# SyncE's reads and stores of finished chunks stand behind the load of pair 36

## The reference

```
x = x + attention(layernorm(x))                       # 16 heads, causal
t = layernorm(x).reshape(4096, 128)
scores = softmax(t @ gate_w.T)                        # 8 experts
_, idx = top_k(scores + gate_bias, 2)
for e in range(8):
    h = silu(t @ w1[e].T) * (t @ w3[e].T)
    y += gate_e[:, None] * (h @ w2[e].T)              # gate_e: the token's weight for e, or 0
z = silu(t @ sw1.T) * (t @ sw3.T) @ sw2.T             # shared experts, all tokens
return x + y + z
```

## Time and profile before

| what | value |
|---|---|
| median of 3 runs | 751.32 us (749.77 to 751.38) |
| the profiled execution, its own time | 750.16 us |
| its span, first to last instruction | 747.3 us |
| mean granted TensorE clock | 0.965 |
| PE, DVE, ACT, POOL busy, share of the span | 83%, 72%, 64%, 62% |

### The profile page before, as it was taken

How to read it: one execution, slowest core, us unless ns; L and a number is a source line. 1 busy time by engine, 2 the same in 40 slices (tenths; PEclk the granted TensorE clock), 3 DMA queues, 4 the chain that set the end, 5 groups by cost and what they waited for, 6 DMA issues and landing times. The chain is left out here.

```text
span 747.3 us, 27456 instructions
## 1 busy us (share of the span) xinstructions
PE 620.2 (83%) x10116; PEld 468.1 (63%) x10116; DVE 537.0 (72%) x1836; ACT 474.7 (64%) x987; POOL 465.7 (62%) x536
## 2 busy tenths in 40 slices
PE   4676978899798999897999988899988678879581
PEld 2354656677576767675677766667765456657461
DVE  7865777788687799886879887888974465425372
ACT  2686977788688868887877887977662232313210
POOL 9453454655446667868655887756587256777652
PEclk9988999999999999999999999999999899989986
DMA  9899998778998876987877886886552534333583
GB/s 255 258 278 321 335 311 261 241 218 257 305 280 248 252 221 185 275 272 206 259 217 217 237 258 211 261 252 190 179 195 66 144 110 108 106 96 105 139 249 86
DMA packets 150227, 161.89 MB, mean 217 GB/s; under 512 B 13676, under 2 KB 115825, under 8 KB 149776
## 3 DMA queue, kind: packets, MB, share of 16 engines
q1 hardware_dynamic: 145488, 151.67, 68.0%
q0 software_dynamic: 4608, 8.47, 3.3%
HBM read 93.87 MB, written 67.26 MB: 216 GB/s over the span
## 5 line engine op out<-in xcount | busy, mean ns | idle before, releaser
L1171 DVE CUSTOM_DVE_ANT_0 ps<-ps,near 128x128 f32<-128x128 f32 (+3 forms) x512 | 244.3, 508 | 73.9 <-PE ps L920 59.3
L1091 ACT ACTIVATE work<-ps,nmin 128x128 f32<-128x128 f32 (+3 forms) x512 | 248.0, 547 | 70.0 <-DVE nmin L1171 62.1
L932 PE MATMUL ps<-ident,work 128*128 128x128 f32 x1280 | 202.7, 277 | 20.1 <-issue 10.2
L932 PEld LDWEIGHTS ps<-ident,work 128*128 128x128 f32 x1280 | 155.0, 142 | 46.4 <-issue 18.5
L871 POOL TENSOR_SCALAR_AFFINE_SELECT work<-work 128x512 f32<-128x512 f32 x96 | 61.3, 639 | 137.8 <-ACT work L1080 108.4
L920 PE MATMUL ps<-kb,qb 128*128 128x128 bf16 (+3 forms) x512 | 130.4, 306 | 14.5 <-ACT work L1091 10.3
L1156 DVE COPY work<-ps 128x512 f32<-128x512 f32 (+1 forms) x192 | 123.1, 641 | 20.7 <-POOL work L875 14.9
L875 POOL TENSOR_TENSOR work<-work 128x512 f32<-128x512 f32 x96 | 124.1, 1293 | 8.0
L1589 POOL DMA_INDIRECT parts<-near x80 | 78.5, 981 | 49.4 <-DVE near L1924 29.6
L1080 ACT ACTIVATE work<-ps 128x512 f32<-128x512 f32 (+1 forms) x160 | 90.0, 563 | 23.1 <-PE ps L932 17.7
L949 PE MATMUL ps<-work,vb 128*9 128x128 f32 x2560 | 95.6, 276 | 6.5 <-ACT relS L1067 2.6
(11 more groups left out here) (172 smaller groups left out, 848.3 us busy)
## 6 DMA issues: line engine op xcount, KB each, us to landing
near<-w_slots SPq DMA_DIRECT2D x96, 512.0 KB, 5.5
w_slots<-relS SPq DMA_DIRECT2D x128, 256.0 KB, 4.2
qk_rows<-work SPq DMA_DIRECT2D x36, 256.0 KB, 4.8
near<-w_slots SPq DMA_DIRECT2D x32, 256.0 KB, 4.1
near<-slots SPq DMA_DIRECT2D x80, 65.0 KB, 2.0
qb<-parts SPq DMA_DIRECT2D x16, 256.0 KB, 3.5
qk_rows<-y SPq DMA_DIRECT2D x9, 256.0 KB, 6.9
qb<-qk_rows SPq DMA_DIRECT2D x24, 96.0 KB
```

Source lines behind the costliest of these rows:

```text
L932: ins = nc.tensor.transpose(tp_ps[:, m % 2, n * P:(n + 1) * P], prob[:, m % PROBS, n * P:(n + 1) * P], ident[:, :])
L1091: ins = nc.scalar.activation(prob[:, m % PROBS, h * wide:(h + 1) * wide], qk_ps[:, m % 3, h * wide:(h + 1) * wide], ACT.Exp, bias=nmin[:, ...
L1171: nc.vector.tensor_tensor_reduce(out=scores, in0=scores, in1=near[:, q % NEAR, a, 4 * P - wide:4 * P, r], scale=1.0, scalar=3e38, op0=ALU. ...
```

## The change

The tables `REST_AT` and `STORE_AT` go; SyncE's rests and stores of lot 0 hang on the loads of pairs 36, 38 and 39 instead, and each store stands ahead of the rest that uses its slot in the order. `FINISH_AT` moves by two steps, to steps 57 to 62 (`LAST_A + NX + 2 + c`). `FREED` is 36, the pair whose load waits for the put of pair 27.

```diff
--- before.py
+++ after.py
@@ -1299,9 +1299,9 @@
 MAP_STEP = (4, 18)
 SPREAD_STEPS = {18 + k: k for k in range(TOPK * GB * NI)}
 LAST_A = max(step for step, j in PAIR_AT.items() if j < PAIRS[0])
-FINISH_AT = {LAST_A + 9 + c: c for c in range(GB * LOTS[0])}
-REST_AT = {LAST_A + (5 + c if c < 2 else 8 + c): c for c in range(GB * LOTS[0])}
-STORE_AT = {step + 1: c for step, c in FINISH_AT.items()}
+FREED = PAIRS[0] + NX - 1
+FINISH_AT = {LAST_A + NX + 2 + c: c for c in range(GB * LOTS[0])}
+REST_BEHIND = {FREED: (0, 1), FREED + 2: (2,), FREED + 3: (3, 4, 5)}
 
 
 def expert_part(nc, ctx, t, ps, x1_done, ynT_done, lgr_done, chain, pj_ready, exp_done, x1_dram, xT_dram, slots, parts, gate_w, gate_bias, w123, out):
@@ -1497,6 +1497,10 @@
             for at, j in PAIR_AT.items():
                 if step == max(at - LEAD, FIRST_PAIR - 1):
                     load_pair(sp, j)
+                    for c in REST_BEHIND.get(j, ()):
+                        if c >= 2:
+                            store_out(sp, c - 2)
+                        load_rest(sp, c)
             if step == MAP_STEP[1] + 2:
                 store_pads(sp, 1)
             for at, (kind, *what) in SHARED_AT.items():
@@ -1505,10 +1509,8 @@
                         load_turned(sp, what[0] + 2)
                     if kind == "product":
                         load_x1(sp, what[0] + 2, wait_stored)
-            if step in REST_AT:
-                load_rest(sp, REST_AT[step])
-            if step in STORE_AT:
-                store_out(sp, STORE_AT[step])
+        for c in range(GB * LOTS[0] - 2, GB * LOTS[0]):
+            store_out(sp, c)
         for c in range(GB * LOTS[0], CHUNKS):
             load_rest(sp, c)
         for c in range(GB * LOTS[0], CHUNKS):
```

## The result

The changed kernel takes 754.27 us (median of 20 runs), the kernel before 751.07 in as many; the ratio is 1.005, with a 95% interval of 1.0029 to 1.0071. It is slower, by about 3.8 us (0.5% of 751). The ratio counts only the runs in the faster of the two states that executions of either kernel fall into, so it is not quite that of the medians, which lie 3.2 us apart. The time lies outside the range (747.6 to 753.4), and the forecast of a small gain did not come true; rival A did.

A forecast was written before the change was run, and what follows sets the result against it. GpSimd's puts waited for `weigh`, held on VectorE by `finish(0)` waiting 6.22 us for rest 0. Gains 0.9 + 0.7 = 1.6 us, less 0.65 for the clock, gave 0.95 off: 751.32 becomes 750.4 us, range 747.6 to 753.4.

The forecast's parts named there:

- forecast of a small gain: Whole kernel: 0.95 us off the profiled execution, the median going from 751.32 to 750.4 us.
- rival A: Pair 37's load lands late and TensorE starts cold: 1.4 us slower, 752.7 us; chance 22%.
- The place and what frees VectorE: Steps 55 to 58: without `finish(0)` in step 55, `weigh` 32 comes near 704.8 and GpSimd's 3.96 us idle goes.
- ceiling of 7.4 us: GpSimd's last 16 put instructions at the old cadence: the last starts at 726.98 instead of 734.42, the most any gain allows.
- Issues of SyncE: Rests 0 and 1 from 700.43, pair 37's load at 703.65 and 704.2, pair 39's at 713.2 and 713.75.
- The step that failed: Pair 37's load, issued behind rests 0 and 1, is little held up and lands at 706.4, on time for turn 37.
- The clock: TensorE idle some 4 us before turn 39, then a step at 1.2 GHz: 1.3 us, half counted, 0.65.
- Pair 39's load: Issued behind store 0 and rest 2, it lands in 2.1 to 2.3 us: turn 39 at 716.0, before 716.86; 0.9 gained.
- From turn 39 to the last put: End of the put chain: 17.8 us instead of 18.5, 0.7 shorter, with `finish(5)` waiting for rest 5.
- the main case: VectorE freed at step 55, the stall moved to TensorE at step 59: 1.6 us gained less 0.65, 750.4 us.
- the point of decision: Sign for rival A: turn 39 comes later than 717.6, 0.7 behind where it stood.

The follow-up runs named there:

- e6: Changed kernel with rest 0 behind pair 36's load, rest 1 behind 38's, the others behind 39's; ratio 0.99 to the kernel before, 0.9948 when run again.
- e2: Changed kernel with pair 39's load ahead of store 0 and rest 2, so it waits for no finish; 747.75 us, ratio 0.995 to the kernel before.
- e4: Changed kernel with the finishes back at their old steps (55 to 60), SyncE's new order kept; 754.68 us, ratio 1.0032 to the kernel before.
- e7: Changed kernel with unused transposes ahead of turns 37 and 39 to keep TensorE busy; ratio 1.0043 to the kernel before, 1.0017 when run again.
- e8: Changed kernel with rests 0 and 1 issued by ScalarE instead of SyncE; 749.3 us, ratio 0.999 to the kernel before.
- e3: Changed kernel with all pairs' loads ahead as before the change, keeping later finishes and store before next rest; 746.53 us, ratio 0.9919 to the kernel before.
- e5: Kernel before with only each store moved ahead of the next rest (all loads ahead, finishes at steps 55 to 60); 752.66 us, ratio 1.0025.

## Why the prediction was wrong

In the order of its steps, with this trace's 0.6 us taken off where a time is compared:

- **The place and what frees VectorE** were right, and no run gained more than the ceiling of 7.4 us (e6: 5.5 of the stretch). `weigh` 32 came at 704.6 (forecast 704.8), `finish(0)` waited for nothing, and GpSimd kept its cadence through pair 32's put.
- **Issues of SyncE** were right to 0.1 us: rest 0, rest 1, pair 37's load, and pair 39's 2.48 behind the end of `finish(0)` (forecast 2.5).
- **The step that failed: "so that of rest 1, issued at 702.5, lands at 705.7 or later, and the load behind it is little held up".** I set the landing of pair 37's load at 2.2 us, from pair 39's load, which had one rest (512 KB) issued ahead of it. With the megabyte ahead it took 4.3, and 4.2 in e2, 5.2 in e4, 4.4 and 4.0 in e7 and its repeat, 4.6 in the changed kernel's repeat: in all six traces with both rests ahead on SyncE (turns 6.1 to 7.5 us apart, against 3.2 to 3.9 with one rest ahead). The 3.2 that I took for the least landing of a second half was rest 2's, issued when rest 1 had all but landed; behind another rest it took 4.9, so rest 1 landed at 707.9 and not at 705.7 + 0.6. And I had read a row wrongly: the 3.8 of pair 37's load in the kernel before was that of its second issue, not of its first, which took 2.1:

```profile
DMA to landing us min/median/max: 2.1/2.1/2.1
```

Read rightly, 704.2 + 3.8 = 708.0 was the value to carry, and it is nearly what was measured (708.5 without the 0.6). That it comes so near is luck in part, since no rest stood ahead of that load; but it was the row of this very load, and it was already late. Turn 37: 709.12 where 706.46 + 0.6 = 707.1 was forecast, 2.0 late. The Trainium skill, "DMA: Bandwidth & Descriptors", section "Queues, rings and completion order", says that each engine consumes the descriptors of one queue in ring order; from that I infer that the load's data wait for the megabyte's. The six traces agree with that; e8, which was to tell it from a mere sharing of the engines, did not, so this part of the cause is argued and not shown.
- **The clock** was counted once, at turn 39, and by half. It fell at both: `weigh` stood 3.7 us behind turn 37 and behind turn 39 instead of 2.5, 1.2 each. I had let turn 37 be on time, so there was no idle of TensorE ahead of it to see. e7 puts both together at 2.7 to 3.0.
- **Pair 39's load** landed 2.7 us after its issue, not 2.2: 0.5 more. Turn 39 came 2.0 + 1.2 + 0.5 = 3.7 later than forecast (719.7 against 716.0).
- **From turn 39 to the last put** 19.0 us instead of 17.8; the 1.2 is the second slow step. `finish(5)` waited for its rest (0.81), as said.

The sum had been 1.6 us better than before without the clock's price; 2.0 + 1.2 + 0.5 + 1.2 = 4.9 worse than that is 3.3 us slower, and the stretch grew by 3.4. Behind the failed step the mechanism of the main case was right in its places, and one term, the landing behind a megabyte, was sized by a row that did not bear it; the clock then added to it. Rival A was this case, at 22%, with the point of decision (turn 39 later than 717.6) where it had to be; its price, 3.0 us where 4.9 came, was still too small, mostly since it counted the clock once. It should have been the forecast, since all its price hung on that one landing, and an estimate for it lay at hand beside the misread row: 1.05 MB at the 252 GB/s of the earlier trace rows take 4.2 us, and only 3.4 lay between the first rest's issue (700.8) and the load's second (704.2).

What the change was good for, moving the finishes, gains 0.8% by itself (e3; in e5, with the finishes back and VectorE's 6.3 us wait with them, nothing is left of it); the two moves on SyncE, each of which puts a bulk transfer ahead of a small load that TensorE waits for, cost more than that. The second of them costs only together with the later finishes: in e4, with the finishes at their old steps, turn 39 came 2.2 us behind turn 38, though store 0 and rest 2 stood ahead of its load there too.

## What to carry to other kernels

In an in-order issue queue, ask of each small load that an engine waits for how many bytes are under way ahead of it, not only when it is issued; a load of two times 65 KB landed 4.0 to 5.2 us after its second issue with 1 MB of rests ahead, and 2.1 to 3.7 with half of that. Read which of two transfers a landing belongs to before you carry it into a sum. Put a transfer that waits for compute behind all loads that don't, even if it is ready "anyway" in the steady state. And each stall of some 4 us on TensorE was paid twice here, the second time in a slow step, so price the clock at each stall and not only at the new one.

## What the runs showed of the hardware

Transposes without use, 28 and 36 of them, kept the granted clock at 1.0 across two stalls and shortened the stretch by 2.7 to 3.0 us. GpSimd's put instruction is not a constant: it takes 0.97 us, but in the changed kernel also 1.24 (714.18, 725.37) and, at 715.73, 1.45. Why is not shown; heavy traffic alone does not do it, since between 703 and 707 us, with the DMA share at 1.05, three of them took 0.97 each. And the program up to pair 36's load, which no edit but e8's touched, took between 690.9 and 708.4 us in fourteen profiles, a spread larger than any effect studied here.
